# Score rows of a multi-stage attention kernel reordered: each load of keys or queries goes to every sixth partition, with six key loads per batch for three

## The reference, cut to what matters

```
q = _split_heads(query @ Wq.T + bq)        # 16 heads of 16 dimensions
k = _split_heads(key @ Wk.T + bk)
v = _split_heads(value @ Wv.T + bv)
scores = jnp.einsum('bhqd,bhkd->bhqk', q, k) / jnp.sqrt(jnp.float32(D_K))
attn = jax.nn.softmax(scores, axis=-1)
ctx = jnp.einsum('bhqk,bhkd->bhqd', attn, v)
return ctx.transpose(0, 2, 1, 3).reshape(B, Sq, D_MODEL) @ Wo.T + bo
```

## Time and profile before

| | |
|---|---|
| time, median of 3 runs | 3417.76 us (3401.97 to 3419.03) |
| the profiled execution's own time | 3407.92 us |
| its span in the trace | 3405.9 us |
| PE busy | 2666.6 us (78%) |
| DVE busy | 1938.7 us (57%) |
| ACT, POOL busy | 1319.5 us (39%), 999.0 us (29%) |
| moved by DMA | 370.64 MB, mean 109 GB/s |
| cross stages, roughly | 346 to 556, 745 to 957, 1600 to 1812, 2533 to 2810 us |
| self stage, roughly | 1389 to 1557 us |

### The profile page before, as it was taken

One profiled execution on the slowest core, in us unless ns is written; L12 is line 12 of the kernel. 1 busy time (PEld: TensorE's weight loads), 2 busy tenths in 40 slices (PEclk: granted clock), 3 DMA queues, 4 the chain that ended last, 5 costly groups with the idle time before them and its releaser, 6 DMA issues. The chain is left out here.

```text
span 3405.9 us, 58910 instructions
## 1 busy us (share of the span) xinstructions
PE 2666.6 (78%) x21336; PEld 2078.4 (61%) x21336; DVE 1938.7 (57%) x3532; ACT 1319.5 (39%) x2568; POOL 999.0 (29%) x859
## 2 busy tenths in 40 slices
PE   7997688958979998594886937786749993699993
PEld 7996466936756665362674624454427772688883
DVE  5555665147753223485765058778856653466773
ACT  4444455234541112364454203333333442355551
POOL 3333100020002222454001024345430003677774
PEclk9998789978979998797887968988879995899997
DMA  7888893468730000865871010000066842455542
GB/s 226 242 243 227 144 157 90 153 125 147 140 126 0 1 0 20 136 67 122 149 137 36 0 74 0 1 0 0 1 132 121 148 75 104 150 193 200 206 180 80
DMA packets 193508, 370.64 MB, mean 109 GB/s; under 512 B 23152, under 2 KB 152816, under 8 KB 179872
## 3 DMA queue, kind: packets, MB, share of 16 engines
q1 hardware_dynamic: 182512, 286.12, 38.4%
q0 software_dynamic: 10800, 81.84, 6.4%
HBM read 271.42 MB, written 96.01 MB: 108 GB/s over the span
## 5 line engine op out<-in xcount | busy, mean ns | idle before, releaser
L934 DVE TENSOR_REDUCE arena<-ps 112x2 f32<-112x750 f32 x512 | 469.7, 935 | 256.7 <-PE ps L819 171.2
L918 ACT ACTIVATE arena<-ps 125x448 f32<-125x448 f32 x768 | 410.2, 545 | 453.9 <-PE ps L837 446.9
L470 POOL TENSOR_SCALAR ln_tmp<-ln_tmp 112x16 f32<-112x16 f32 x11 | 2.9, 263 | 1287.5 <-DVE ln_tmp L438 1287.5
L819 PE MATMUL ps<-wreg,arena 96*112 96x375 bf16 x768 | 235.5, 374 | 134.1 <-DMA arena<-query_parts 98.2
L2337 PE MATMUL ps<-moe_x_r,moe_w_r 128*128 128x256 f32 x2016 | 255.0, 287 | 27.8 <-DVE arena L2455 26.3
L2337 PEld LDWEIGHTS ps<-moe_x_r,moe_w_r 128*128 128x128 f32 x2016 | 247.4, 193 | 32.4 <-issue 29.5
L837 PEld LDWEIGHTS ps<-arena,wreg 98*125 98x125 bf16 x2304 | 215.9, 144 | 74.7 <-issue 30.3
L837 PE MATMUL ps<-arena,wreg 98*125 98x112 bf16 x2304 | 238.7, 229 | 12.5 <-DMA arena<-arena 7.8
L2267 POOL TENSOR_TENSOR moe_w_r<-wreg,moe_w_r 128x512 fp32r<-128x512 f32 x160 | 220.5, 1403 | 35.6 <-ACT moe_w_r L2365 33.9
L1941 POOL TENSOR_TENSOR arena<-arena 112x1024 f32<-112x1024 f32 x64 | 156.6, 2454 | 227.8 <-DVE arena L2055 161.4
L492 PE MATMUL ps<-ident,xn 112*128 112x112 f32 x320 | 72.1, 380 | 182.4 <-DVE xn L451 138.2
(11 more groups left out here) (300 smaller groups left out, 5841.6 us busy)
## 6 DMA issues: line engine op xcount, KB each, us to landing
key_parts<-arena SPq DMA_DIRECT2D x128, 281.2 KB, 3.9
wreg<-key_parts SPq DMA_DIRECT2D x48, 562.5 KB, 7.1
arena<-query_parts SPq DMA_DIRECT2D x108, 224.0 KB, 10.9
values<-arena SPq DMA_DIRECT2D x64, 357.0 KB
arena<-values SPq DMA_DIRECT2D x64, 357.0 KB
wreg<-key_parts SPq DMA_DIRECT2D x48, 375.0 KB, 8.3
query_parts<-arena SPq DMA_DIRECT2D x48, 336.0 KB, 2.5
wreg<-in_e_w SPq DMA_DIRECT2D x16, 704.0 KB, 5.3
```

What stands on the lines that cost most here:

```text
L819: mm = pe.matmul(ps[0:T, 2 * (p % 2) + e, 0:S2], queries(b)[0:SROWS, hd, :], keys[r][0:SROWS, hd, :], start=True, stop=not masked)
L918: act.activation(probs[k % PROBS], ps[0:KN, 4 + k % 2, 0:GT], ACT.Exp, scale=scale).then_inc(at_probs, 1)
L934: dve.tensor_reduce(negmax[r % 2][:, 2 * p:2 * p + 2], ps[0:T, 2 * (p % 2):2 * (p % 2) + 2, 0:S2], AX.X, ALU.max, negate=True).then_inc(at ...
```

## The change

The row of product j and dimension d moves from 16 j + d to 6 d + j, for keys and queries alike, so the contraction sums the same 96 products. `spread(j)` is every sixth partition from j on. A load of 16 rows that went to 16 neighbouring partitions now goes to partitions j, j + 6, ..., j + 90. The key loads of 48 and 32 rows become three and two loads of 16 rows each, since their parts no longer lie together: six key loads of 187.5 KB a batch in place of three. Bytes, sources, buffers, waits and the order of the loads are as before, except that `arrived` waits for six. In `self_stage` the number of loads stays at 12.

```diff
-K_RUNS = ((0, 3), (3, 2), (5, 1))
+K_PART = (0, 1, 2, 0, 1, 0)
 Q_PART = (0, 0, 0, 1, 1, 2)
 SROWS = DH * len(Q_PART)
 AROWS = SROWS + 2
+
+
+def spread(j):
+
+    return slice(j, SROWS, len(Q_PART))
+
@@
         def load_keys(sp, keys, kv, b, r):
-            for at, parts in K_RUNS:
-                sp.dma_start(keys[DH * at:DH * (at + parts), :, :].rearrange("p h k -> p (h k)"),
-                             key_parts[kv, b, 0:parts].rearrange("q (d h) k -> (q d) (h k)", d=DH)).then_inc(at_loaded[r], 16)
+            for j, q in enumerate(K_PART):
+                sp.dma_start(keys[spread(j), :, :].rearrange("p h k -> p (h k)"),
+                             key_parts[kv, b, q].rearrange("(d h) k -> d (h k)", d=DH)).then_inc(at_loaded[r], 16)
@@
                     for j in which:
-                        sp.dma_start(group_q[g % 2][DH * j:DH * j + DH, :, :],
+                        sp.dma_start(group_q[g % 2][spread(j), :, :],
@@
-                    pe.wait_ge(at_loaded[r], (turn + 1) * (16 * len(K_RUNS)))
+                    pe.wait_ge(at_loaded[r], (turn + 1) * (16 * len(K_PART)))
@@
-                    for at, parts in K_RUNS:
-                        for q in range(parts):
-                            sp.dma_start(group_k[u][DH * (at + q):DH * (at + q + 1), :, :],
-                                         query_parts[1, q, :, cols].rearrange("(d h) n -> d h n", d=DH)).then_inc(group_in[u], 16)
+                    for j, q in enumerate(K_PART):
+                        sp.dma_start(group_k[u][spread(j), :, :],
+                                     query_parts[1, q, :, cols].rearrange("(d h) n -> d h n", d=DH)).then_inc(group_in[u], 16)
                     for j, q in enumerate(Q_PART):
-                        sp.dma_start(group_q[u][DH * j:DH * j + DH, :, :],
+                        sp.dma_start(group_q[u][spread(j), :, :],
```

## The result

The changed kernel takes **3329.49 us** (median of 4 runs, 3319.53 to 3333.03), the kernel before 3415.44 beside it (4 runs, 3401.97 to 3419.03). The ratio is **0.9746**, 95% interval 0.9724 to 0.9768: 2.5% faster, where 3.0% was forecast. The profiled execution took 3333.03 us, 74.9 us less than that of before; its span in the trace is 3331.1 us, 74.8 less.

The account below looks back on a forecast made before the run. PE was taken to bound ordinary steps but to wait for slow key and query loads at stage starts and in steps 6 and 10. Gains of 26 + 13 + 56 = 95 us gave 3314 us, range 3288 to 3356.

Parts of the forecast that it names:

- estimate of 325 GB/s: First query loads of a batch: by the skill page's port figures, all six spread loads take 3.5 us, about 325 GB/s.
- Starts of the cross stages: First query loads, four stages: 4.7 us in place of 11.2, 6.5 us less each, 26 us in all.
- 293 GB/s: Rate assumed for spread key and query loads, taken from the values' loads to 112 partitions; queries had 123.
- Self stage: Start of the self stage: faster loads gain 13 us, then POOL's mask chain, ending at 1406.37, is late next.
- Steps 6 and 10: Eight long steps of the cross stages: the load backlog and its waits vanish, clock included, gaining 56 us.
- from 201 GB/s on nothing is late: Query steps: keys and queries, 1.84 MB, have 9.15 us beside the values, so 201 GB/s suffices.
- the 64.9: Excess in us of the eight long steps, 159.24, over ordinary ones, 94.4; 8.5 of it was expected to stay.
- Three more key loads: SP's extra issues per batch, at 0.42 us each: six end at 486.9, before the maxima at 487.17; cost 0.
- The two stops without a releaser: Stops of 4.93 and 3.57 us where PE waits for nothing shown; left out of the gain as possibly staying.
- Rival 1: Hidden stops keep about 5 us per long step, or rate is near 200; 3325 to 3355 us; 2 in 10.
- Rivals 2 and 3: 2: only key loads faster, about 3352 us (1 in 20); 3: rates unchanged, 3410 to 3420 us (1 in 20).
- Rival 4: Any 16-row load goes at 123 GB/s wherever its rows lie, keys too; about 3490 us; 6 in 100.

Follow-up runs that it names:

- number 1: Changed kernel with rows back in the old order: six key loads and six query loads, each to 16 neighbouring partitions; 3458.29 us, ratio 1.0118 to the kernel before.
- number 2: Changed kernel with only the query loads spread, keys in their three neighbouring loads as before; 3374.38 us, ratio 0.9872 to the kernel before.
- number 3: Changed kernel with only the key loads spread, queries on 16 neighbouring partitions as before; 3387.17 us, ratio 0.9905 to the kernel before.
- number 4: Changed kernel with loads to every second partition in place of every sixth, each spanning 31 partitions; 3343.94 us, ratio 0.9763 to the kernel before.
- Number 7: Changed kernel with ACT issuing three of the six loads of each cross stage's first query group; 3334.25 us, ratio 0.9721 to the kernel before.
- number 11: Number 6's kernel with each cross stage's first query group loaded in two halves, batches 0 and 1 first; 3316.72 us, ratio 0.9698 to the kernel before.
- Number 6: Changed kernel with all six loads of the next query group issued in steps 4 and 8; 3329.71 us, ratio 0.9711 to the kernel before.
- number 12: As number 11, but with halves in the unmasked stages only; 3325.55 us, ratio 0.968 to the kernel before.

## Why the prediction was right, and where it was off

**The cause was right.** Rows on neighbouring partitions slow a load (numbers 1 to 4), and the share of DMA engines hides it: it was 1.16 at 123 GB/s and 1.01 at 228. The rate does not go with a load's span (number 4). In the kernels that load every sixth partition, the same two windows gave 238 to 251 GB/s for keys and, where whole query groups come first, 228 to 243 for queries; every second partition gave 222 and 223, every fourth 233 and 217.

The map of the Trainium skill (SBUF — State Buffer, Door 1: The DMA port swizzle) puts 16 neighbours on 4 ports, every second or fourth row on 8, every sixth on 13 or 14. These runs agree in order: 121 to 131 for queries on neighbours, 217 and 223 on 8 ports, 228 to 243 on 13. They don't agree in size: the prediction's estimate of 325 GB/s from the page's figures was not reached, and 13 ports were little better than 8. That the ports are the shared thing is argued from this order; a simpler rule, that it is enough to leave a gap between a load's rows, would explain all but the small differences among the spread patterns, and no run tests it.

The size of the pieces may matter as well, which I had ruled out by a store: among neighbours, keys went at 172 and queries at 131. No run changes the size of the pieces alone.

**Starts of the cross stages** (26 us forecast, 18.0 measured). The mis-sized term is the rate. I took 293 GB/s because a spread load spans nearly as many partitions as the values; number 4 shows that this reason was wrong, since a span of 31 gave 223. 1.376 MB take 11.2 us at 123 and 6.0 at 228: 5.2 us a stage; measured are 4.5, 4.5, 4.3 and 4.6. Number 7 shows that the issues don't hold it, number 11 that the bytes do. POOL's memsets stayed hidden, as forecast.

**Self stage** (13 and 10.95). POOL's mask chain was to be late next. It ends at 1366.30 + 4.75 = 1371.05 and PE starts at 1373.45, so the loads still end last, by 2.4 us, at 220 GB/s. The mis-sized term is the rate again.

**Steps 6 and 10** (56 and 50.0). Here a step of the argument failed, though its size came out near: "from 201 GB/s on nothing is late". The rate was 228 to 238, and six waits of 0.72 to 2.96 us stayed, 9.6 us in all; in two of these steps the mean granted clock was 0.88 and 0.79 besides. The criterion compared the bytes of a step with its length: at these rates 4.8 us for keys, 1.4 for values and 3.0 for queries, 9.2 of 10.55. What decides is when the last load is issued and how long it then takes to land: the issue ended at 439.75, and PE, which wanted the data 1.63 us ahead of 443.36, that is at 441.73, got it 3.61 us after that issue. Number 6 shows it: the same bytes at 233 to 244 GB/s, all issued a step earlier, and the query waits are gone. Number 2 shows the other side: transfers of 11.0 us in a step of 10.55, 0.9 us over in two steps, and waits of up to 6.50. A sum of bandwidth near the length of the step leaves nothing for the time to land.

That 50.0 came out near 56 is partly luck. The forecast left 8.5 us of stops in and took everything else of the 64.9 away. Measured, the stops went too, but 14.9 us of the excess stayed, in waits and clock.

**Three more key loads** (0 forecast). "They just fit" was worked out with 0.42 us an issue, and a spread one takes 0.589: six took 3.7 us and not 2.5, in step 5 even 4.50. The same step of the kernel before, whose keys start at 433.32:

```profile
436.30 1.21 SPq L783 DMA_DIRECT2D arena<-arena  x2
...
438.62 1.93 SPq L773 DMA_DIRECT2D arena<-query_parts  x3
```

The maxima are issued 4.55 us after the first key load, where it was 2.98, and the last query issue ends 9.61 us after it, where it was 7.23. Those 2.4 us are more than the wait of 1.63. So this cost may well be inside the waits that stayed in the long steps; no run takes it away by itself. The maxima themselves were never waited for. The split without spreading costs 1.2% (number 1). In its trace the cross stages, from first to last key load, are 27.0 us longer than before; PE's waits and stops in the whole trace are 17.6 us more: 103.1 us of waits for queries for 98.2, 13.5 in 12 waits for the maxima for 7.8 in 5, and 19.3 of stops for 12.3. How the rest divides is not shown.

**The two stops without a releaser** The earlier trace rows that I left out of the sum are gone; PE's stops of this kind over 0.5 us add up to 12.3 us before and to none after. The ordinary steps became 5.7 us shorter, which the sum had at nothing, and 2.7 of that were such stops. Together these brought the gain back up where the rate and the landing fell short. Such stops go with full queues: 19 us in number 1, stops up to 3.83 us in number 2, only one, of 0.53, in number 3. But number 12 has one of 2.20 behind the start of its second cross stage. That PE's instructions come late behind the data in the queues would explain them; it is argued, not shown.

**The rivals.** Rival 1 was half right: something did remain in the steps, but it was the landing of the last queries and not a stop behind them, 9.6 us and not 40. The measured time, 3329.49, lies in this rival's range of 3325 to 3355 as well as in the forecast's gain of 80 to 115 us; the trace decides between them. Rivals 2 and 3 fall, since queries went from 123 to 228. Rival 4 had a false premise: number 1 shows that even neighbouring 16-row key loads go at 172, not 123.

**What stays open**: why spread loads stop at 217 to 251 GB/s where the values behind them went at 293 before, what holds the issue of a spread key load up by 0.17 us, and when a short wait takes the clock down with it.

## What to carry to other kernels

If a window shows the DMA engines fully busy at a low rate, look at which partitions the load writes before looking at its size: every second partition was nearly enough here (222 GB/s), and a wider spread brought little more (at most 251). Whether a load is in time is read from its last issue plus its time to land (4.6 us median, 3.5 at least), not from bytes against the length of a step. Moving its issue one step earlier took away what the change had left of query waits, for waits of 0.7 to 1.2 us on the small loads behind it. Once the bytes ahead of the first matmul set a start, let it wait for the part that it needs, but see which other load stands behind the pieces.

## What was unexpected of the hardware

- The same key load of 16 rows took SP 420 ns to issue on neighbouring partitions and 589 ns on every sixth one; query loads took 618 and 609.
- Neighbouring loads of 16 rows went at 172 GB/s in pieces of 12,000 bytes and at 131 in pieces of 896; spread over every sixth partition, both went at 228 to 251.
- Every second, fourth and sixth partition gave 217 to 251 GB/s; the sixth was the highest throughout, and between second and fourth there is no order (222 and 223, 233 and 217).
- PE's stops without a shown releaser, 12.3 us in all, were gone after the change.
